# Adding the two choices' attention outputs on GpSimd, so that one projection per head group serves both

## The reference

```python
logits = x @ router_w + router_b
probs = softmax(logits)
_, top2 = top_k(probs, 2)
for e in range(4):                        # E = 4 experts, 16 heads of 8 features each
    member = (top2 == e).any(-1)
    ...                                   # the member tokens are gathered, the rest is masked
    q, k, v = (xg @ wq[e] + bq[e]), (xg @ wk[e] + bk[e]), (xg @ wv[e] + bv[e])
    att = softmax(where(valid, (q @ k.T) * 0.5, -1e9))
    y = (att @ v) @ wo[e] + bo[e]
    out[order] += wg * y                  # wg: the router's probability of that expert
x = layernorm(x + out)
```

## Time and profile before

| | before |
|---|---|
| time, median of 3 runs | 1452.36 us (1451.96 to 1455.44) |
| profiled execution: span from first to last instruction | 1481.8 us |
| PE / PEld busy | 1231.5 (83%) / 742.3 (50%) |
| DVE busy | 964.4 (65%) |
| ACT busy | 734.6 (50%) |
| POOL busy | 663.4 (45%) |
| mean granted TensorE clock | 0.878 of full speed |

### The profile page before, as it was taken

The page is one execution under the profiler, slowest core; times in us unless marked ns, Lnnn a source line. Parts: engine busy times, 40 slices in busy tenths (PEclk is TensorE's granted clock), DMA queues, the critical chain, the costliest instruction groups (busy, mean ns, idle before and its releaser), DMA issues.

```text
span 1481.8 us, 30563 instructions
## 1 busy us (share of the span) xinstructions
PE 1231.5 (83%) x11664; PEld 742.3 (50%) x11664; DVE 964.4 (65%) x2280; ACT 734.6 (50%) x1244; POOL 663.4 (45%) x1054
## 2 busy tenths in 40 slices
PE   5878786567667889999998998999899888988985
PEld 2555575455223344555555554555555455555543
DVE  4787532255357887777776868677777766757534
ACT  3654432233342456665665656556565554553531
POOL 3376342563167454464443626345363432443430
PEclk7998798797665889999998989999999998998978
DMA  9801465561010001101020110101102010110110
GB/s 337 335 21 34 133 184 161 166 181 54 19 29 23 23 2 40 29 16 38 8 44 8 37 32 13 44 4 42 32 14 43 4 42 15 31 39 9 34 35 8
DMA packets 69480, 87.52 MB, mean 59 GB/s; under 512 B 22062, under 2 KB 54104, under 8 KB 65880
## 3 DMA queue, kind: packets, MB, share of 16 engines
q1 hardware_dynamic: 65240, 77.18, 18.0%
q0 software_dynamic: 4096, 8.40, 1.9%
HBM read 52.16 MB, written 32.21 MB: 57 GB/s over the span
## 4 chain that ended last, share of the span: by engine, by line
PE 41%; DVE 28%; SPq 7%; ACT 7%; issue 6%; POOL 5%; DMA 3%; another core or an unknown queue 2%; ACTq 0%; DVEq 0%; POOLq 0%
PE ps L1677 19%; DVE mneg_e L1492 8%; PE ps L1757 7%; PE ps L864 5%; PE ps L1780 3%; DVE mneg_l L1492 3%; SPq L1141 2%; PE ps L960 2%; SPq L1137 2%; DVE q L1547 1%; PE ps L972 1%; SPq L1159 1%; POOL q_low L1224 1%; PE ps L1777 1%
## 5 line engine op out<-in xcount | busy, mean ns | idle before, releaser
L1335 ACT ACTIVATE probs<-ps 128x1024 f32<-128x1024 f32 x384 | 390.0, 1024 | 260.8 <-PE ps L1677 257.2
L1492 DVE TENSOR_REDUCE mneg_e<-ps 128x2 f32<-128x512 f32 x512 | 337.1, 685 | 66.1 <-PE ps L1677 63.1
L1677 PE MATMUL ps<-k_high,q_high 32*128 32x256 f16 x1024 | 164.3, 286 | 51.0 <-DVE mneg_e L1492 41.1
L1492 DVE TENSOR_REDUCE mneg_l<-ps 128x2 f32<-128x512 f32 x256 | 167.8, 682 | 57.3 <-PE ps L1677 56.1
L1757 PE MATMUL ps<-probs,v_e 128*32 128x256 f32 x2048 | 141.6, 395 | 8.2 <-ACT v_e L1360 4.7
L1677 PE MATMUL ps<-q_high,k_high 32*128 32x256 f16 x1024 | 142.1, 278 | 4.0 <-ACT probs L1335 3.3
L1677 PE MATMUL ps<-q_low,k_high 32*128 32x256 f16 x1024 | 141.4, 275 | 0.0
L1677 PE MATMUL ps<-q_high,k_low 32*128 32x256 f16 x1024 | 140.3, 273 | 0.0
L1677 PE MATMUL ps<-kT,qT 32*128 32x256 f16 x512 | 75.9, 285 | 35.6 <-DVE mneg_e L1492 16.7
L1677 PEld LDWEIGHTS ps<-k_high,q_high 32*128 32x128 f16 x1024 | 54.4, 93 | 97.4 <-DVE mneg_e L1492 62.8
L1288 POOL TENSOR_TENSOR on_e<-o_e,on_e 128x512 f32<-128x512 f32 x60 | 75.7, 1274 | 60.1 <-DMA on_e<-scratch_e 60.1
(11 more groups left out here) (245 smaller groups left out, 2553.6 us busy)
## 6 DMA issues: line engine op xcount, KB each, us to landing
by_expert<-expert_w SPq DMA_DIRECT2D x12, 1536.0 KB, 14.4
expert_w<-in_expert_w SPq DMA_DIRECT2D x48, 321.0 KB
on_e<-scratch_e SPq DMA_DIRECT2D x60, 256.0 KB, 4.8
tokens<-by_expert SPq DMA_DIRECT2D x48, 128.0 KB
by_expert<-y_tokens SPq DMA_DIRECT2D x48, 128.0 KB
on_l<-scratch_l SPq DMA_DIRECT2D x128, 32.0 KB, 1.8
sums_l<-o_l SPq DMA_DIRECT2D x128, 2.0 KB
q_high<-shiftT_e SPq DMA_DIRECT2D x128, 2.0 KB
```

The source lines that it names most:

```text
L1335: act.activation(probs[:, probs_slot(r, i)].rearrange("p j s -> p (j s)"), s_banks(i).rearrange("p j s -> p (j s)"), ACT.Exp, scale=0.5 if ...
L1492: v.tensor_reduce(to, tiles(max_bank(k)), axis=AX, op=ALU.max, negate=True).then_inc(kind.max_used, 1)
L1677: return pe.matmul(o, l, r, start=start, stop=stop)
```

## The change

The four experts now have fixed rows: expert e of a head has rows 8e to 8e+7 whichever choice it is. Choice 0 uses rows 0 to 23 and has its row of sums at 24; choice 1 uses rows 8 to 31 and has its sums at 0. For that, `v_e` holds per head experts 0, 1, 2, ones, experts 1, 2, 3 (56 columns instead of 48), and ACT fills it with two copies of 24 columns per head instead of one of 32. After POOL has normalized a group of both choices it adds choice 1 to choice 0 in place, after a wait for its own multiplication (`link`). PE projects the sum with one `wo` for all four experts: 4 products per block instead of 8. The unused normalized sums (a one in each choice) are cancelled through the bias: `bv` has -1 in the row ONE for experts 0 and 3. SP's row of sums and the tables `sel_sum` and `sel_weight` follow the new rows. The last sequence still projects both choices, now with the shared `wo`.

```diff
-        wo = sb("wo", [P, CHOICES, G, D])
+        wo = sb("wo", [P, G, D])
-        bv = sb("bv", [P, CHOICES, G, ROUTE])
+        bv = sb("bv", [P, G, ROUTE])
-            v_e = sb2("v_e", [P, 2, T, H, ROW + 2 * HD])
+            v_e = sb2("v_e", [P, 2, T, H, 7 * HD])
...
-                                row, to = ROW * j + 3 * HD * c, ROW * j + 16 * c
+                                row, to = ROW * j + 3 * HD * (1 - c), ROW * j + 16 * c
...
-                        pool.tensor_tensor(on_e[:, :, g], o_e[:, :, g], on_e[:, :, g], ALU.mult).then_inc(E.on_ready, 1)
+                        link(pool.tensor_tensor(on_e[:, :, g], o_e[:, :, g], on_e[:, :, g], ALU.mult))
+                        pool.tensor_tensor(on_e[:, 0, g], on_e[:, 0, g], on_e[:, 1, g], ALU.add).then_inc(E.on_ready, 1)
...
-                        act.copy(v_e[:, b % 2, t, :, HD:HD + E1 * HD], x1.rearrange("p (h x) -> p h x", h=H))\
+                        experts = x1.rearrange("p (h x) -> p h x", h=H)
+                        act.copy(v_e[:, b % 2, t, :, 0:C * HD], experts[:, :, 0:C * HD])
+                        act.copy(v_e[:, b % 2, t, :, (C + 1) * HD:(2 * C + 1) * HD], experts[:, :, HD:E1 * HD])\
                            .then_inc(s.v_ready, 1)
...
-                            values = (v_e[:, b % 2, t, J * blk + j, 2 * HD * c:2 * HD * c + ROW] if kind is E
+                            values = (v_e[:, b % 2, t, J * blk + j, C * HD * c:C * HD * c + ROW] if kind is E
...
                         mm(x0[:, 0:D], routeT[:, b % 4, t * P:(t + 1) * P], bo[:], stop=False)
-                        for c in range(CHOICES):
-                            for g in range(G):
-                                last = mm(x0[:, 0:D], on_e[:, c, g, t * P:(t + 1) * P], wo[:, c, g, :], start=False,
-                                          stop=c == CHOICES - 1 and g == G - 1)
+                        for g in range(G):
+                            last = mm(x0[:, 0:D], on_e[:, 0, g, t * P:(t + 1) * P], wo[:, g, :], start=False, stop=g == G - 1)
                         last.then_inc(E.out_ps, 1)
...
-                                    last = mm((x0, x1)[t][:, 0:D], last_on[:, c, g, t * P:(t + 1) * P], wo[:, c, g, :], start=False,
+                                    last = mm((x0, x1)[t][:, 0:D], last_on[:, c, g, t * P:(t + 1) * P], wo[:, g, :], start=False,
```

More of the change, by code:

```diff
@@ L1916, in slot @@
                         take(6, const1_ready, 3)
[L1917 to L1920, removed]
+                        for g in range(G):
+                            last = pe.matmul(x0[0:ROUTE, 0:D], bv[:, g, :], wo[:, g, :], start=g == 0, stop=g == G - 1)
                         last.then_inc(const1_ready, 1)
@@ L2023, with of_choices @@
     c = np.ascontiguousarray
-    def of_choices(x, shift=0):
+    def of_choices(x):
         heads = x.reshape(x.shape[:-1] + (G, J, 1, HD))
@@ L2030, in of_choices @@
             parts = np.concatenate([heads[choice + k] for k in range(C)], axis=-2)
-            if shift and choice == 0:
-                parts = np.concatenate([np.zeros_like(heads[0]), parts], axis=-2)
             choices.append(rows_of_heads(parts))
@@ L2039 @@
     bk[..., SHIFT_E] = 1.0
-    wo = of_choices(c(f["L1_ffn_wo"].transpose(0, 2, 1)), shift=1)
+    wo = f["L1_ffn_wo"].reshape(E1, G, J, HD, D).transpose(2, 0, 3, 1, 4)
     wproj = np.zeros((2, J, 2, PACK, D), np.float32)
@@ L2049 @@
         for j in range(J):
-            sel_sum[j, 3 * HD * choice, choice, j] = 1.0
+            sel_sum[j, 3 * HD * (1 - choice), choice, j] = 1.0
         for k in range(C):
@@ L2054 @@
             sel_pick[(FIRST, SECOND)[choice] + e, choice, :, PICK_ROW + k] = 1.0
-            at = (1 - choice) * HD + k * HD
+            at = (choice + k) * HD
             sel_weight[(FIRST_W, SECOND_W)[choice] + e, choice, :, at:at + HD] = 1.0
             sel_mask[KEY_MASK + e, choice, :, PICK_ROW + k] = 1.0
-        at = 3 * HD * choice
+        at = 3 * HD * (1 - choice)
         sel_weight[ONE, choice, :, at:at + HD] = 1.0
@@ L2062 @@
     bo[SECOND_W:SECOND_W + E1] = f["L1_ffn_bo"]
-    bv_rows = np.zeros((CHOICES, G, J, ROW, ROUTE), np.float32)
+    bv_rows = np.zeros((J, E1, HD, G, ROUTE), np.float32)
     for e in range(E1):
-        choice = 0 if e < C else 1
-        at = (1 - choice) * HD + (e - choice) * HD
-        values = f["L1_ffn_bv"][e].reshape(G, J, HD)
-        bv_rows[choice, :, :, at:at + HD, FIRST_W + e] = values
-        bv_rows[choice, :, :, at:at + HD, SECOND_W + e] = values
+        values = f["L1_ffn_bv"][e].reshape(G, J, HD).transpose(1, 2, 0)
+        bv_rows[:, e, :, :, FIRST_W + e] = values
+        bv_rows[:, e, :, :, SECOND_W + e] = values
+    bv_rows[:, 0, :, :, ONE] = -1.0
+    bv_rows[:, E1 - 1, :, :, ONE] = -1.0
     def by_head(x):
@@ L2093 @@
         "wv": c(by_head(f["L1_ffn_wv"])),
-        "wo": c(wo.transpose(3, 4, 1, 2, 0).reshape(P, CHOICES, G, D)),
+        "wo": c(wo.reshape(P, G, D)),
         "wqkv": f["L1_attn_W_qkv"],
@@ L2097 @@
         "bq": c(bq.transpose(2, 3, 0, 1).reshape(P, CHOICES, G)), "bk": c(bk.transpose(2, 3, 0, 1).reshape(P, CHOICES, G)),
-        "bv": c(bv_rows.transpose(2, 3, 0, 1, 4).reshape(P, CHOICES, G, ROUTE)),
+        "bv": c(bv_rows.reshape(P, G, ROUTE)),
         "bo": bo,
```

## The result

| | before | after |
|---|---|---|
| time, median of 20 runs | 1451.55 us (1437.02 to 1457.90) | 1456.64 us (1450.25 to 1470.17) |
| ratio to before, 95% interval | 1 | 1.0053 [1.0032, 1.0074] |
| mean granted clock over the timed runs | 0.8935 (35 runs of the next series; 0.8906 and 0.8933 in two more) | 0.8669 |

By the ratio the kernel became 7.7 us slower (0.53% of 1451.55, by the interval 4.6 to 10.7 us; the medians are 5.1 apart), where 8.4 us faster was forecast. PE has half of the products and is granted a lower clock.

The account below looks back on a forecast made before the run. No single engine bounds the kernel: PE has 41% of the chain, DVE 28%. -15.4 - 3.2 + 5.6 + 4.6 = -8.4 us, from 1452.4 to 1444.0 us; eight-in-ten range 1424 to 1469, the forecast's own 1436 to 1453.

Parts of the forecast that it names:

- Slot 6: PE's block of products in slot 6: half of 2.05 us goes and the gain is kept, 15 x 1.03 = 15.4 us.
- Slot 2: PE's block in slot 2: nearly no gain, as DVE's reciprocal in slot 4 awaits the sums' DMAs; 9 x 0.35 = 3.2 us.
- the wait that it foresaw in slot 4: DVE's reciprocal of the softmax sums waits for its DMA in most periods, for about a microsecond.
- ACT's second copy: Evacuation 0.37 us longer, on the path in slot 0, nothing in slot 4: 5.6 us loss; bounds nothing and twice 5.6.
- POOL's additions: 0.73 us each on POOL, hidden before k_high is needed, except in two late periods: 2 x 2.3 = 4.6 us loss.
- The rival of the low clock: PE idles more; low stretch around slots 5 to 7, 3.9 us a period; six periods give +15, 1467 us; chance 0.30.
- All of PE's time counts: Rival: sums land earlier without a profile, half of PE's 89.0 us goes; -34 us, 1418 us; chance 0.10.

Follow-up runs that it names:

- before, again: The kernel before, run once more with no edit for a second profile (span 1448.9 us): 1450.36 us, ratio 0.9986.
- the run with two queues: Against the kernel after: choice 1's four of the eight transfers of the softmax sums issued from ACT's queue instead of SP's; 1431.80 us, ratio to before 0.9832.

## Why the prediction was wrong, step by step

**Slot 6 failed.** "Half of the block, 2.05 / 2 = 1.03 us, goes ... so the gain is kept: 15 x 1.03 = 15.4 us", and of the clock: "I count them at the same 1.03." The half goes only where the clock stays up (1.16 us in the period from 789.84). Where the block runs at 0.50, in 5 of the eleven periods, it takes 2.08 us and nothing goes; in 3 more it takes 1.16 but begins over a microsecond later. With slot 2's 3.2, 18.6 us were counted for the products; 5 to 8 were measured. The forecast's two steps were not independent: the wait that it foresaw in slot 4 leaves PE without work just ahead of slot 6. Putting work there brought back 15.6 us, and 2.0 in the kernel before. That a wait of 2.17 us left the clock up in the period from 789.84 is not explained, nor is the share of the late periods known.

**Slot 2 was right** in that the sums came last, and its consequence was filed under a rival. The waits of DVE for the sums, after, then before, again:

```profile
  DVE inverse_e L1607: 5.6, 9
```

```profile
  DVE inverse_e L1604: 6.0, 6
```

9 waits, in most of the 15 periods and for some 0.6 us each, where about a microsecond was foreseen. In sum they are no longer than the 6.0 us of before, again (the earlier trace rows had 3.6), so the proof that the sums held the path is the run with two queues and not this row.

**ACT's second copy was mis-sized.** The copies take 0.48 us each, as estimated, but the second starts before the first has ended (0.86 us for both), so the pair is longer by 0.27 and not 0.37. Groups by line, after:

```profile
L1362 ACT COPY v_e<-ps 128x384 f32<-128x384 f32 x32 | 15.3, 478 | 35.7 <-PE ps L1680 35.7
...
L1363 ACT COPY v_e<-ps 128x384 f32<-128x384 f32 x32 | 15.5, 485 | 0.0
```

Still it cost 10.6 to 13.5 us where 5.6 were counted (bound: 11.2). The place was right, slot 0 and not slot 4; about half of the price is unexplained.

**POOL's additions were right** in place and roughly in size. 0.73 us each, hidden in an ordinary period: `k_high` ends at 1122.31, 1.8 us ahead of PE.

```profile
1116.40 0.73 POOL L1289 TENSOR_TENSOR on_e<-on_e 128x256 f32<-128x256 f32 x1
...
1121.70 0.61 POOL L1230 CAST k_high<-k 128x512 f16<-128x512 f32 x1
...
1124.11 0.27 PE L1680 MATMUL ps<-k_high,q_high 32*128 32x256 f16 x1
```

And shown in a late one, where PE stood still until `k_high` ended at 1302.42 (the profile puts the wait down to "issue"):

```profile
1301.81 0.61 POOL L1230 CAST k_high<-k 128x512 f16<-128x512 f32 x1
...
1302.52 0.26 PE L1680 MATMUL ps<-k_high,q_high 32*128 32x256 f16 x1 [2.99 <-issue]
```

4.6 us were counted; 2.0 (after against the kernel without additions, within the noise of the two) and 6.5 (alone, 1.3 to 11.7) were measured.

**The rival of the low clock came true**, in 8 of eleven periods, at about half its price: of after's first ten full periods (the eleventh has fewer instructions) the seven with the fall last 60.9 to 66.2 us, 62.6 on average, the three without it 60.7, a difference of 1.9 us and not 3.9. Its working counted three periods with the fall in the first trace of before; there are four (796.05, 861.32, 1174.74 and 1240.18). The low clock reached the late periods too (0.91 to 0.81), which the rival left out. Against it stood that "the shift by a microsecond can as well move the idle time to where the clock does not fall"; three periods did that.

**The sum, as measured**, along one way through the table: halved products -4.9, second copy and new rows +10.6, additions +2.0, together +7.7 us, against -18.6, +5.6 and +4.6. "All of PE's time counts" got nothing as the kernel stood; with the sums on two queues the change's 18 us go that way.

## What to carry to other kernels

Work taken from PE in front of a wait that stays need not be a gain: ask how long PE then stands idle, and price the next block at either clock. Take away the wait first, here eight small issues on one queue, and then the work. Before believing a loss in the clock, fill the wait with useless products, in both kernels: the two runs tell it from a loss in the path.

## What was not expected of the hardware

- Twelve useless matrix instructions a period (1.60 us in one of them) made the kernel 15.6 us faster, at a clock of 0.887 instead of 0.867 over the timed runs.
- Runs of one and the same kernel differ in their mean clock (before, in the last series of 29: 0.884 to 0.905), and the time goes with it, 9.5 to 12.3 us for 0.01 in three series.
- Four DMA issues on each of two queues take 2.74 and 2.44 us side by side, eight on one queue 5.00.
